# Cross-attention values of two pairs of key tiles multiplied in one place instead of two

## What is computed

```python
sa_out = merge(softmax(causal(q @ k.T * scale)) @ v) @ sa_wproj + sa_bproj   # self-attention
result = tgt + sa_out
xq, xs = layernorm(result), layernorm(src)                                   # src: 750 context tokens
k2, v2 = split(xs @ ed_wkv);  q2 = xq @ ed_wq
wei2   = softmax(q2 @ k2.T * scale)                                          # 224 x 750, 16 heads, 8 sequences
result = result + merge(wei2 @ v2) @ ed_wproj + ed_bproj                     # cross-attention
result = result + relu(layernorm(tgt) @ ff_w1 + ff_b1) @ ff_w2 + ff_b2
```

## Time and profile before

| what | value |
|---|---|
| time, median of 3 runs | 1370.09 us (1369.25 to 1372.01) |
| span of the profiled execution | 1372.2 us (its time with what lies around the span is not listed) |
| PE busy | 1310.9 us, 96% |
| DVE, ACT, POOL busy | 58%, 48%, 51% |
| granted PE clock | 0.984 on average, 1.00 in the steps looked at below |
| cross-attention | about 750 to 1372 us, groups of four steps that repeat every 80.9 us |

### The profile page before, as it was taken

One profiled execution on the slowest core, in us unless ns is written; L12 is line 12 of the kernel. 1 busy time (PEld: TensorE's weight loads), 2 busy tenths in 40 slices (PEclk: granted clock), 3 DMA queues, 4 the chain that ended last, 5 costly groups with the idle time before them and its releaser, 6 DMA issues.

```text
span 1372.2 us, 24578 instructions
## 1 busy us (share of the span) xinstructions
PE 1310.9 (96%) x9193; PEld 1082.5 (79%) x9193; DVE 794.4 (58%) x2007; ACT 662.1 (48%) x1609; POOL 701.5 (51%) x577
## 2 busy tenths in 40 slices
PE   7999999999899999998788999999999999999997
PEld 6888888888788888887677787878877787887874
DVE  6613223232777777776655575756757566575565
ACT  5311111232666665666433656474665647456444
POOL 3232221322444555556733767666676766667661
PEclk9999999999999999999599999999999999999999
DMA  7400102114647776547267685777677587766641
GB/s 237 145 18 16 62 31 77 46 60 117 139 86 178 166 186 148 122 123 185 63 142 119 100 128 98 132 123 125 101 127 120 101 137 104 142 101 112 90 71 41
DMA packets 100400, 151.67 MB, mean 111 GB/s; under 512 B 10197, under 2 KB 63229, under 8 KB 99514
## 3 DMA queue, kind: packets, MB, share of 16 engines
q1 hardware_dynamic: 100282, 150.11, 53.8%
HBM read 66.74 MB, written 24.12 MB: 66 GB/s over the span
## 4 chain that ended last, share of the span: by engine, by line
PE 76%; POOL 8%; issue 5%; DVE 5%; DMA 3%; ACT 2%; SPq 1%; POOLq 0%; ACTq 0%; DVEq 0%
PE ps L1727 18%; PE ps L453 11%; PE ps L164 10%; PE ps L423 10%; PE ps_pair L1744 6%; PE ps L1759 5%; PE ps L1773 5%; PE ps L1832 3%; POOL ca_partial L1586 2%; DMA ca_k_stack<-ca_keys 2%; POOL ca_xT L1473 1%; DMA sa_K_stack<-sa_rows 1%; PE ps L1207 1%; PE ps L1791 1%; PE ps L1227 1%
## 5 line engine op out<-in xcount | busy, mean ns | idle before, releaser
L1664 DVE TENSOR_REDUCE ca_maxes<-ps 112x1 f32<-112x375 f32 x512 | 256.5, 541 | 106.0 <-PE ps L1759 103.9
L1607 ACT ACTIVATE ca_probT<-ps_pair 125x448 f32<-125x448 f32 x384 | 210.3, 554 | 181.5 <-PE ps_pair L1744 179.6
L1586 POOL TENSOR_TENSOR ca_partial<-ca_partial,ca_probT 125x896 f32<-125x896 f32 x118 | 249.2, 2112 | 93.6 <-ACT ca_probT L1607 89.0
L312 POOL TENSOR_TENSOR ff_hT<-ff_hrelu,ff_hT 128x512 fp32r<-128x512 f32 (+1 forms) x64 | 77.9, 1218 | 203.2 <-DVE ff_hT L394 203.2
L1759 PE MATMUL ps<-ca_k_stack,ca_q_stack 96*112 96x376 f32 x512 | 168.7, 352 | 6.9 <-issue 3.6
L1744 PEld LDWEIGHTS ps_pair<-ca_q_stack,ca_k_stack 98*125 98x125 f32 x768 | 130.2, 186 | 44.0 <-issue 31.9
L1744 PE MATMUL ps_pair<-ca_q_stack,ca_k_stack 98*125 98x224 f32 x768 | 156.2, 285 | 1.3 <-ACT ca_probT L1607 1.2
L423 PE MATMUL ps<-ff_w,ff_hT 128*128 128x512 f32 x672 | 155.5, 390 | 0.0
L1727 PE MATMUL ps<-w_b,ca_xT 128*125 128x512 f32 x576 | 151.2, 398 | 3.1 <-POOL ca_xT L1473 2.5
L1727 PE MATMUL ps<-ca_xT,w_a 128*128 128x376 f32 x768 | 153.1, 335 | 0.0
L423 PEld LDWEIGHTS ps<-ff_w,ff_hT 128*128 128x128 f32 x672 | 125.6, 188 | 25.8
(11 more groups left out here) (145 smaller groups left out, 2433.0 us busy)
## 6 DMA issues: line engine op xcount, KB each, us to landing
ca_k_stack<-ca_keys SPq DMA_DIRECT2D x96, 376.0 KB, 8.0
sa_Q_stack<-sa_rows SPq DMA_DIRECT2D x96, 112.0 KB, 3.5
sa_K_stack<-sa_rows SPq DMA_DIRECT2D x96, 112.0 KB, 3.7
ca_q_stack<-q_out SPq DMA_DIRECT2D x96, 112.0 KB, 9.5
ctx_tokens<-in_ctx_dram SPq DMA_DIRECT2D x14, 672.0 KB
ctx_tokens<-in_L_xattn_ff_w_dram SPq DMA_DIRECT2D x16, 512.0 KB, 4.4
q_out<-sa_yT SPq DMA_DIRECT2D x16, 448.0 KB, 3.7
wp_lo<-wp_out SPq DMA_DIRECT2D x6, 1024.0 KB, 4.8
```

Of the source, the lines that this page charges most:

```text
L312: pool.tensor_tensor(hT[:, LO, m % RING, 0:width(g)], hrelu[i % 2][:, 0:width(g)], hT[:, HI, m % RING, 0:width(g)].bitcast(F32), ALU.subtr ...
L1586: pool.tensor_tensor(total, total, half(a), ALU.add).then_inc(partial_done, 1)
L1607: act.activation(probT[u // GH][0:JT, u % GH].rearrange("p a t -> p (a t)"), ps_p[u % 2][0:JT, 0:2 * T], ACT.Exp).then_inc(exp_done, 1)
L1664: dve.tensor_reduce(maxes[:, q, j, a:a + 1], ps_s[n % 3][0:TQ, 0:JH], AX_X, ALU.max).then_inc(s_read, 1)
```

## The change

The item `value` of pair 1 goes from slot 10 of step s to slot 3 of step s + 1, straight ahead of the `value` of pair 2 and of D. Pair 0 stays in slot 7. All other items keep their places, and no instruction is added or taken away.

```diff
+FIRST_VALUES = 7
@@
             if i == 3 and 0 <= s - 4 < NG:
-                items.append(("value", s - 4, 2))
+                items += [("value", s - 4, pair) for pair in (1, 2)]
@@
-            if i in (7, 10) and 0 <= s - 3 < NG:
-                items.append(("value", s - 3, (i - 7) // 3))
+            if i == FIRST_VALUES and 0 <= s - 3 < NG:
+                items.append(("value", s - 3, 0))
```

## The result

| | before | changed |
|---|---|---|
| median of 4 runs | 1371.05 us (1369.25 to 1373.16) | 1384.24 us (1382.12 to 1387.86) |
| ratio | | 1.0098, 95% interval 1.0087 to 1.0110 |
| span of the profiled execution | 1372.2 us | 1380.3 us (its time: 1382.12 us, the shortest of the four) |

The change makes the kernel 13.2 us slower. 8.7 us slower was forecast, 1378.8 us with a range to 1384.0; the median lies just above that range. The sign was right, and so was the size of most steps; a term was missing: stretches in which PE was granted its lower clock.

A forecast was written before the change was run, and what follows sets the result against it. PE was taken as the bound where slot 3 pays, with DVE or ACT limiting slot 10's return for g = 1, 2 and 3. Added 23.2 us less 14.5 back gives +8.7, 1378.8 us; range 1371.5 to 1384 (8 in 10).

The forecast's parts named there:

- What slot 3 takes: Slot 3 of steps 4 to 34: 16 more matmuls cost 0.75 us in each of 31 steps, 23.2 us in all.
- g = 3: Slots 4 to 11: ACT is the bound; only 0.05 us of a wait for POOL comes back, 0.3 us over six steps.
- g = 0: Slot 10: PE is free to go on, so 1.08 us come back in each of six steps, 6.5 us.
- g = 1: Slots 10 and 11: PE waits for DVE's score reads; 0.15 us back in six steps, 0.7 in step 29.
- g = 2: Slots 10 and 11: prob waits for ACT's exponential; 0.35 us back in six steps, 0.7 in step 30.
- PE's waits for L1651 and L1473: Sign in the changed kernel's trace: with g = 3 these waits grow by about 1 us a step.
- The last steps: Steps 32, 33 and 34 give back 0.3, 0.76 and 0.76 us.
- the values of pair 1 would run beside the last exponential: Step 34: pair 1's values no longer stand between ACT and its last prob; 0.76 us back.
- PE as the bound everywhere: Rival: each of 31 steps gains 0.33 us and the end 0.76; 1359.6 us, 0.75% faster; chance 0.09.
- ACT's chain absorbing the shift: Rival: with g = 3 ACT catches up in slots 4 and 5, six steps cost nothing; 1374.6 us; chance 0.12.
- The keys' DMA: Rival: after a shorter g = 0 slot 10, slot 1's cast waits; up to 6.5 us lost, 1385 us; chance 0.08.
- The runs do merge: Rival claimed the opposite in slot 3: PE pays 0.15 us again in 31 steps; 1383.5 us; chance 0.03.

The follow-up runs named there:

- e1: Pair 1 moved to slot 3 only out of steps with g = 0, against the kernel before: 0.9991.
- e2: Pair 1 moved to slot 3 only out of steps with g = 1 and g = 2, against the kernel before: 1.0051.
- e11: Changed kernel with three of six statistics per context (slots 9 to 11, g = 1) over 32 of 512 channels; against the kernel before 1.0068.
- e5: Changed kernel with the value projections of slots 8 and 9 (g = 1, g = 2) put into slots 9 and 10; against the kernel before 1.0039.
- e17: Changed kernel with DVE making the float32 copies and POOL's slot 7 sum behind slot 8's low part (g = 3); against the kernel before 1.0047.
- e6: Kernel before with only the value projections moved from slots 8 and 9 to 9 and 10, pair 1 staying in slot 10: 1.0026.
- e13: Kernel before with pair 1 moved only for g = 0 and 1, not from step 32 on; g = 1 value projection in slots 9 and 10: 0.9974.
- e8: Kernel before with the second read of each transposed context tile (float32 copy) on DVE instead of ACT: 1.0007.
- e15: Kernel before with POOL's sum of slot 7 put behind the low part of slot 8 with g = 3: 1.0027.
- e3: Pair 1 moved to slot 3 only out of steps with g = 3, against the kernel before: 1.0053.
- e16: Changed kernel with pair 1 left in slot 10 in steps 32 to 34; against the kernel before 1.0075, 1382.7 us.
- e7: Changed kernel with the second read of each transposed context tile (float32 copy) on DVE instead of ACT; against the kernel before 1.0076.
- e14: Changed kernel with POOL's sum of slot 7 put behind the low part of slot 8 with g = 3; against the kernel before 1.0071.
- e9: Changed kernel with the low part of one context tile in eight taken by DVE instead of POOL; against the kernel before 1.0114.
- e10: Kernel before with the low part of one context tile in eight taken by DVE instead of POOL: 1.0063.
- e12: Kernel before with pair 1 moved only for g = 0 and 1, g = 1 value projection in slots 9 and 10, low part on DVE: 1.0054.

## Why the prediction was right, and where it fell short

**What slot 3 takes.** 0.75 us a step. Right: the window behind each moved step grows by 0.74 or 0.75 (e1, e2), by 0.65 behind g = 3, where 0.05 of a wait for POOL goes too, as said, and 0.05 more.

**What slot 10 gives.** g = 0: 1.08 forecast, 1.07 measured. g = 1: 0.15 and 0.12, with DVE's queue as the cause (e11) and 1.13 if PE has other work (e5). The scores there are full-width products, so this is DVE's queue and not a case of tiling. g = 3: nothing, as forecast; but ACT isn't the bound alone there, POOL stands beside it (e17). g = 2: 0.35 and 0.17: here a term of the sum was too large. In the changed kernel's timeline slot 10's exponential starts 0.80 us later behind slot 3, 0.05 more than the shift; prob of slot 0 follows it after 0.68 us instead of 0.97, 0.29 gained and not 0.35; and the first prob of slot 1 loses another 0.07. Six such steps: 1.1 us.

**The missing term.** This is the step that failed. The table of the kernel before has the clock as "1.00 in the steps looked at below", and the prediction never asked whether the change would alter it. It named the growth of PE's waits itself ("PE's waits for L1651 and L1473 with g = 3 grow by about 1 us a step"; measured are 0.84) and priced it at nothing. The first trace, the fastest of its four executions, has two such stretches inside cross-attention, 1.54 us in step 19 and 1.34 in step 34: 2.9 us. The repetition's trace, its slowest execution, has four (steps 3, 15, 27 and 34), 6.1 us. Over all traces, for the steps 7 to 27 with g = 3:

| g = 3 steps of | PE idle in such a window | with half clock |
|---|---|---|
| before, e1, e6, e13 | 1.1 us | 0 of 24 |
| e2, e8, e15, e17 | 0.75 to 1.15 us | 0 of 24 |
| changed kernel (twice), e3, e5, e11, e16 | 1.9 to 2.0 us | 7 of 36 |
| e7, e14 | 1.6 to 1.8 us | 1 of 12 |
| e9, e10, e12 | 1.8 to 2.0 us, 1.5 of it in one wait | 11 of 18 |

Among these steps the stretches come only where PE waits longer, wherever the values stand. Step 34 shows that the idle time of a step isn't the whole rule, since there it didn't grow. What decides in which of these steps the clock falls, these runs don't show.

**The last steps** were forecast 0.3 us shorter and are 0.7 shorter at full clock; what makes the changed kernel's traces longer there is the clock again. The claim that the values of pair 1 would run beside the last exponential was right:

```profile
1367.16 0.98 ACT L1608 ACTIVATE ca_probT<-ps_pair 125x448 f32<-125x448 f32 x2 [0.37 <-PE ps_pair L1745]
1367.27 1.89 PE L1774 MATMUL ps<-ca_probT,ca_v 125*32 125x224 f32 x32
1368.97 0.54 PE L1792 MATMUL ps<-ca_partial,ca_ones 125*32 125x224 f32 x2
```

The last exponential ends at 1368.14 and D starts 0.83 us behind it; before, it ended at 1360.00 and D started 0.84 us behind it, at 1360.84. Pair 1 costs nothing there. Steps 32, 33 and 34 give back 0.37, 0.93 and 0.87 us in e5 against e6, where 0.3, 0.76 and 0.76 were forecast.

**The sum.** Steps 4 to 7: +1.7 forecast, +1.85 measured (first trace). Steps 8 to 27: +6.9 and +7.7, and the clock's 1.5 on top. Steps 28 to 31: -0.2 and -0.3. From slot 3 of step 32 on: +0.4 and +1.4, of which the clock is 1.3. Together +8.8 and +12.2. With all half-clock stretches of cross-attention taken off, those at the very end too (1.0 us in both traces, by e6 and e5), it is 614.0 and 623.3 us: +9.3 where +8.8 was forecast. The repetition comes to the same 623.3. So the steps were summed right within 0.6 us, with g = 2 1.1 us too low and the last steps 0.4 too high, and the clock adds 2.9 us in one trace and, with its shorter end, 5.4 in the other. The medians' 13.2 lies between 9.3 + 2.9 and 9.3 + 5.4; how many stretches the other executions had isn't known.

**The rivals.** PE as the bound everywhere (0.09) fell with e2 and e3. Its price has a slip, without effect: 31 x 0.33 + 0.76 is 11.0 us, not 10. ACT's chain absorbing the shift (0.12) fell with e2, whose g = 3 window takes up 0.76 us. The keys' DMA is waited for, without loss (e1). The runs do merge: slot 3's 40 matmuls take 2.03 us, as forecast.

The range failed by 0.24 us: it was widened for terms of the sum that might be off, and had no room for a cost outside of it. That the miss is so small is in part luck, since the stretches differ in number from one execution to the next.

## What to carry to other kernels

Before work is moved out of a place to save PE time, read what PE does next there: if it only has instructions whose inputs another engine is still making, the time saved turns into a wait, while the place that receives the work pays in full. When an engine in front of PE is relieved and nothing happens, look for a second chain that ends at nearly the same time before dropping the theory. Where a change moves or lengthens PE's waits, in a stretch in which it waits already, put the lower clock into the sum as a cost of its own. And before two traces' lengths are compared, see that the granted clock is the same in both: here the last steps looked up to 0.7 us slower by the change and are 0.7 us faster.

## What the runs showed of the hardware

- Going from full-width to 32-column matmuls and back costs 0.33 us a time: with the move out of a full slot, 1.07 us are saved for 0.75 us of matmuls (e1). The Trainium skill's rule that a change of tiling mode drains TensorE (TensorEngine Tiling (Array Packing), Key Properties) agrees with it. The runs show the price in this kernel, 0.33 us, and not the drain itself.
- PE was granted 1.2 GHz behind a stretch in which it still was busy for 3.20 of 5.10 us and never waited longer than 0.72 us at a time, and in step 34 behind waits of 0.30 us at most. The same stretches stand in steps that kept 2.4 GHz.
- The same subtraction of a 128x375 tile took 0.98 us on POOL and, on DVE, 0.54 us with POOL idle and 1.95 us when it started while POOL ran a sum of two SBUF tiles (e10).
